# Fused cross-attention and mixture-of-experts kernel: another VectorE order in the attention steps, one undivided row-scatter pair, and batch 15's gate, output and statistics ahead of tile 0

## Chip, cores and metric

One core of one Trainium2 chip runs the kernel. The metric is the device time in microseconds of one execution. All input preparation (transposes, splitting into blocks, constant tables) happens before it.

## What is computed

`x` has 16 batches of 128 tokens with 128 features; a context of the same 16 x 128 tokens has 256 features. Cut to what matters:

```python
x = x + tanh(g_xattn) * xattn(ctx, layernorm(x), mask, mask, W_src, b_src, W_tgt, b_tgt, W_out, b_out)
x = x + tanh(g_ffn) * ffn(layernorm(x), w1, w2, w3, new_w1, new_w2, new_w3, gate, gate_bias)
# xattn: 8 heads of 16, keys and values from ctx, queries from x, masked softmax,
#        then W_out on [layernorm(x), attention result]
# ffn:   scores = sigmoid(x @ gate.T + bias) over 9 experts, the top 2, weights divided by their sum;
#        out = sum over experts of weight * ((silu(x @ w1.T) * (x @ w3.T)) @ w2.T), hidden size 352
```

## The kernel before

The kernel writes every engine's instruction list out by hand and joins the engines with semaphores. It has three stages.

**Projections** (to about 38 us) are not touched.

**Attention steps.** `turns(step)` runs steps k = 0 to 16 on PE, ACT, DVE and POOL; each engine has its own `step(k, r, i)` with r = k mod 4. Step k works on batch k's scores, on batch k-1's probabilities, on batch k-2's output and on batch k-3's normalised rows, so one step carries a quarter of the chain of four batches. On PE (L1189) the order within a step is: score products of batch k (L1178, then the mask bias L1185), `turn_out(k-2)` (L1258), the eight probability transposes of batch k-1 (L1216), `turn_rows(k)` (L1269 and L1275), the products with the values (L1228), and `gate_and_out(k)` (L1283 and L1285). On ACT: two copies of the transposed probabilities, the copy of the turned rows (L448), four exponentials (L405), the copy of the value products (L427), four exponentials.

DVE's step (L877) is, in order: the first row maxima (L829), `unturn` (a reciprocal L835 and a product L839), `norm2` of batch k-3 (L848), the second maxima, then the routing work of the step if there is some, then `second` of batch k-2 (L869, L871, L875: add the output product to x, and the statistics of the layer norm). `norm2(b)` waits for `rs2` of batch b, which POOL makes (L567, L569) from the statistics of `second(b)`.

The **routing** of a group of four batches is spread over steps by `routed(k, r, at)`, which gives group g when k = at + 4g. DVE's parts: `logits_of` and `clamp` at k = 6, 10, 14; `make_keys` and `choose` (`find_top`, `mark_top`: which two experts) at k = 7, 11, 15; `weigh`, `keep_ranks`, `place_rows` and `label_rows` (which row of which expert each token goes to) at k = 8, 12, 16. PE's `rank(g)` (L1234) counts the tokens by expert, inside `turn_rows` at k = 8, 12, 16, behind five or eight filler products (`keep_busy`, L1248). Every small DVE operation of the routing is followed at once by a wait for itself (`route_link`).

POOL's step (L540) is: scale the values of batch k (L545), `rstd2_of(k-3)`, the first copy of a scatter of 128 rows to `x_rows` (L597, for group g and place p at k = 9 + 4g + p), `keep(k-3)` (a copy of the normalised rows, which waits for `norm2`), and the scatter's second copy. `scatter` waits for `label_set` of its group.

**Tables.** `table_counts` and `table_rows` (L923, L948) turn the counts into the row and the expert of each of 40 tiles. `table_rows(0)` for the first 8 tiles runs at k = 14, its `table_counts(0)` at k = 13. After the last step DVE does `unturn(15)`, `norm2(14)`, `table_used(0)` and `table_counts(1)`.

**Tiles.** 40 tiles of 128 rows, each of one expert, run through a pipeline over k: SyncE loads the tile (L299 to L312 for the first eight), PE transposes it (L1334), ACT and DVE split it into two parts, PE multiplies with w1 and w3 (L1323 to L1325), ACT and DVE make the hidden rows, PE transposes and multiplies with w2 (L1374, L1365), ACT scales the result (L477) and POOL scatters it to `y_rows` (L620). The routing of the last group of batches is mixed into tiles 0 to 9 (`within`, `between`). SyncE's list ahead of tile 0 is: wait for `rows_known`, four loads of row numbers into registers (L304), wait for the scatters of the groups before, then the tile loads.

```python
                rows = [sp.value_load(row_of[0:1, n * TR + r:n * TR + r + 1], min_val=0, max_val=NE * CAP) for r in range(AHEAD)]
                for p in range(UN):
                    sp.wait_ge(st_rows[p], (NG - len(EARLY) + n) * 32)
```

Of the kernel before, what the change touches and what calls it, by code (L numbers as in the profile page):

```python
# [18 lines left out]
ALU = mybir.AluOpType  # L19
# [7 lines left out]
P = 128  # L27
NB = 16
# [32 lines left out]
LOWS = {1: (0, 1, 2), 2: (3,), 3: (4,), 4: (5,), 5: (6,), 6: (7,), 9: (8,)}  # L61
# [7 lines left out]
def build(nc, x, ctxT, mask, first, consts, row_consts, w_srcT, w_tgtT, w_outT, w13T, w2T, gateT, x_rows, y_rows, out):  # L69
    with ExitStack() as ctx:  # L70
# [171 lines left out]
        def in_switch(k):  # L242

            return k == SWITCH

# [254 lines left out]
        def _(pool):  # L500
# [39 lines left out]
            def step(k, r, i):  # L540
# [102 lines left out]
        def _(dve):  # L643
# [84 lines left out]
            route_links = {}  # L728
            LINKS = {"clamp": 1, "keys": 4, "choose": 3, "weigh": 4, "place": 2}

            def route_link(g, stage_name, ins):

                route_links[stage_name] = route_links.get(stage_name, 0) + 1
                before = sum(n for name, n in LINKS.items() if list(LINKS).index(name) < list(LINKS).index(stage_name))
                ins.then_inc(route_chain, 1)
                dve.wait_ge(route_chain, g * sum(LINKS.values()) + before + route_links[stage_name])

            def clamp(g):

                route_links.clear()  # L740
                dve.wait_ge(lg_kept, g + 1)
                nc.vector.tensor_scalar(logits[:, 0:GZ], z[:], FLOOR, None, ALU.max).then_inc(lg_ready, 1)
                route_link(g, "clamp", nc.vector.tensor_scalar(key[:].rearrange("p b e -> p (b e)"), z[:], FLOOR, KNEE, ALU.max, ALU.min))
                assert route_links["clamp"] == LINKS["clamp"]

            def add_one(g):

                route_links.clear()
                dve.wait_ge(sig_exp, g + 1)
                route_link(g, "keys", nc.vector.tensor_scalar(sigs[:], sigs[:], 1.0, None, ALU.add))  # L750
                route_link(g, "keys", nc.vector.reciprocal(sigs[:], sigs[:]))

            def above_knee(g):

                knee = sigs[:, GZ:GZ + 1]
                route_link(g, "keys", nc.vector.tensor_scalar(over[:], sigs[:, 0:GZ], knee, knee, ALU.max, ALU.subtract))
                flat_key = key[:].rearrange("p b e -> p (b e)")
                route_link(g, "keys", nc.vector.scalar_tensor_tensor(flat_key, over[:], STRETCH, flat_key, ALU.mult, ALU.add))
                assert route_links["keys"] == LINKS["keys"]

            def make_keys(g):

                add_one(g)
                above_knee(g)

            def find_top(g):

                route_links.clear()
                for b in range(UN):
                    last = nc.vector.max(top[:, b, :], key[:, b, :])  # L770
                route_link(g, "choose", last)
                for b in range(UN):
                    last = nc.vector.max_index(top_at[:, b, :], top[:, b, :], key[:, b, :])
                route_link(g, "choose", last)

            def mark_top(g):

                last = nc.vector.tensor_tensor(choices[:], part["experts"].unsqueeze(1).unsqueeze(1).to_broadcast([P, 2, UN, NE]),
                                               top_at[:, :, 0:2].rearrange("p b c -> p c b").unsqueeze(3).to_broadcast([P, 2, UN, NE]), ALU.is_equal)
                route_link(g, "choose", last)  # L780
                assert route_links["choose"] == LINKS["choose"]
# [3 lines left out]

            def choose(g):

                find_top(g)
                mark_top(g)
# [6 lines left out]
            def weigh(g):  # L796

                route_links.clear()
                dve.wait_ge(chosen, g + 1)
                route_link(g, "weigh", nc.vector.tensor_tensor(flat_of, flat_choices, of_choices(sigs[:, 0:GZ]), ALU.mult))  # L800
                route_link(g, "weigh", nc.vector.tensor_reduce(sel_sig[:], chosen_of[:], AX.X, ALU.add))
# [679 lines left out]
```

## Time and profile before

| What | us |
|---|---|
| median of 3 runs (lowest, highest) | 215.69 (215.64, 215.78) |
| the profiled execution | 215.48 |
| its span, first to last instruction | 213.7 |
| PE, DVE, ACT, POOL busy | 201.5, 147.7, 142.3, 128.4 |
| mean granted TensorE clock | 0.994 of full speed |

The profiled execution lies 0.2 us below the median. Its own time is 1.8 us more than its span. PE's busy time counts matmuls whose ends are modelled, so it also covers short waits.

### The profile page before, as it was taken

Reading aid. Unit: us, or ns where it says so; the run is one execution under the profiler, and the core shown is the slowest. Engines: PE = TensorE matmul, PEld = TensorE weight load, DVE = VectorE, ACT = ScalarE, POOL = GpSimd, SP = SyncE. Lnnn points to the kernel's source line nnn. Section 1 sums busy time; section 2 is a strip of 40 time slices with the busy share of each in tenths; the row PEclk is TensorE's granted clock in tenths of the full one; section 3 lists DMA queues with packets and bytes.
Section 4 is the critical chain, followed back from the end, with each engine's and each line's share of the span. In section 5 each row is a group of like instructions: output and inputs, shape, how many; then the busy total and the mean of one; then the engine's idle time right before and its main releaser. Section 6 shows DMA issues by size and latency. Waiting matters only on the chain.

```text
span 213.7 us, 5788 instructions
## 1 busy us (share of the span) xinstructions
PE 201.5 (94%) x1606; PEld 162.8 (76%) x1606; DVE 147.7 (69%) x523; ACT 142.3 (67%) x399; POOL 128.4 (60%) x230
## 2 busy tenths in 40 slices
PE   8999998999999999999979899999999999999972
PEld 2676575576766676676648789999999999998971
DVE  0269979877889969899977997534444344467583
ACT  2355896999886888678746757576666767666110
POOL 5226657023342588677767867888888887567120
PEclk9999999999999999999999999999999999999997
DMA  5997999999993001000024823232222222261394
GB/s 151 380 391 208 366 408 406 404 398 344 312 349 92 14 28 37 25 28 26 28 70 122 234 64 96 69 87 76 66 77 72 60 64 62 66 225 33 87 354 155
DMA packets 23601, 34.91 MB, mean 163 GB/s; under 512 B 2561, under 2 KB 15878, under 8 KB 23442
## 3 DMA queue, kind: packets, MB, share of 16 engines
q1 hardware_dynamic: 20610, 29.27, 40.9%
q0 software_dynamic: 2240, 4.23, 6.3%
q10 hardware_dynamic: 720, 1.02, 1.6%
q8 instruction: 15, 0.25, 0.5%
q14 instruction: 16, 0.13, 0.2%
HBM read 15.85 MB, written 19.06 MB: 163 GB/s over the span
## 4 chain that ended last, share of the span: by engine, by line
PE 61%; DVE 18%; POOL 6%; issue 5%; ACT 5%; DMA 3%; POOLq 0%; SPq 0%; DVEq 0%; ACTq 0%
PE pt_ps L1365 10%; PE score_ps L1323 5%; PE pt_ps L1374 5%; PE score_ps L1325 5%; PE score_ps L1324 5%; PE score_ps L1178 4%; PE pt_ps L1118 4%; PE ps_a L1228 3%; PE pt_ps L1216 3%; PE score_ps L1128 3%; DVE less L829 2%; DMA kheads<-y_rows 2%; ACT probs L405 2%; PE ps_a L1334 2%; POOL y_rows L620 2%
## 5 line engine op out<-in xcount | busy, mean ns | idle before, releaser
L620 POOL DMA_INDIRECT y_rows<-vals,ids x38 | 37.7, 993 | 11.2 <-ACT vals L477 4.4
L405 ACT ACTIVATE probs<-score_ps,less 128x128 f32<-128x128 f32 x128 | 37.4, 405 | 1.7 <-DVE less L829 1.7
L597 POOL DMA_INDIRECT x_rows<-stage,slot x32 | 32.6, 1020 | 9.2 <-issue 7.7
L1365 PE MATMUL pt_ps<-w,probsT 128*128 x234 | 32.6, 275 | 0.9 <-DVE probsT L1018 0.6
L1365 PEld LDWEIGHTS pt_ps<-w,probsT 128*128 128x128 f32 x234 | 30.8, 190 | 1.6 <-issue 1.4
L477 ACT ACTIVATE vals<-pt_ps,xg 128x128 f32<-128x128 f32 x38 | 13.9, 367 | 26.6 <-PE pt_ps L1365 26.6
L1045 DVE TENSOR_TENSOR xg_low<-ps_a,xg_high 128x128 fp32r<-128x128 f32 x40 | 11.6, 290 | 28.8 <-ACT xg_high L459 28.4
L1323 PE MATMUL score_ps<-w_high,xg_low 128*128 x80 | 29.2, 365 | 0.0
L1325 PE MATMUL score_ps<-w_high,xg_high 128*128 x80 | 25.9, 323 | 0.0
L1324 PE MATMUL score_ps<-w_low,xg_high 128*128 x80 | 25.6, 320 | 0.0
L1053 DVE TENSOR_TENSOR probs<-probs,score_ps 128x352 f32<-128x352 f32 x40 | 20.8, 520 | 6.4 <-ACT probs L466 3.6
L829 DVE TENSOR_REDUCE less<-score_ps 128x4 f32<-128x512 f32 x32 | 21.7, 684 | 3.0 <-PE score_ps L1185 2.9
L466 ACT ACTIVATE probs<-score_ps 128x352 f32<-128x352 f32 x40 | 18.6, 464 | 1.3 <-PE score_ps L1325 1.2
L1374 PE MATMUL pt_ps<-fst,probs 128*128 128x128 f32 x117 | 19.2, 273 | 0.1
L484 ACT COPY probsT<-pt_ps 128x384 f32<-128x384 f32 x38 | 18.2, 478 | 0.3 <-PE pt_ps L1374 0.2
L1178 PE MATMUL score_ps<-kheads,qT 64*128 64x256 f32 x128 | 18.2, 402 | 0.2
L1216 PE MATMUL pt_ps<-fst,probs 128*128 128x128 f32 x128 | 17.1, 274 | 1.0 <-ACT probs L405 1.0
L567 POOL TENSOR_SCALAR ve<-mv 128x1 f32<-128x1 f32 x16 | 3.7, 231 | 22.8 <-DVE mv L875 22.8
L1216 PEld LDWEIGHTS pt_ps<-fst,probs 128*128 128x128 f32 x128 | 14.4, 141 | 2.0 <-ACT probs L405 1.9
L1323 PEld LDWEIGHTS score_ps<-w_high,xg_low 128*128 128x128 f32 x80 | 15.1, 189 | 0.5 <-issue 0.2
L1324 PEld LDWEIGHTS score_ps<-w_low,xg_high 128*128 128x128 f32 x80 | 15.2, 190 | 0.0
L1325 PEld LDWEIGHTS score_ps<-w_high,xg_high 128*128 128x128 f32 x80 | 15.0, 187 | 0.0
(179 smaller groups left out, 442.8 us busy)
## 6 DMA issues: line engine op xcount, KB each, us to landing
x_rows<-pads SPq DMA_DIRECT2D x1, 9945.0 KB, 37.2
w_low<-in_w13T SPq DMA_DIRECT2D x3, 1056.0 KB, 10.5
xg<-x_rows SPq DMA_DIRECT2D x40, 65.0 KB, 1.8
ctx_r<-in_ctxT SPq DMA_DIRECT2D x4, 512.0 KB, 7.1
y_rows<-pads SPq DMA_DIRECT2D x1, 2048.0 KB, 18.1
w<-in_w2T SPq DMA_DIRECT2D x1, 1728.0 KB, 12.6
kheads<-y_rows SPq DMA_DIRECT2D x3, 512.0 KB, 5.2
mask_b<-in_mask SPq DMA_DIRECT2D x4, 256.0 KB, 7.5
```

The costliest lines, as they stand in the source:

```text
L405: last = nc.scalar.activation(probs[:, r % 2, h, :], score_ps[:, r % 2, h, :], ACT.Exp, bias=less[:, r % 2, h:h + 1])
L597: pool.indirect_dma_start(x_rows[:, :], bass.IndirectOffsetOnAxis(ap=slot[:, par, c, p:p + 1], axis=0), stage[:, par, c, p, :], None, boun ...
L620: pool.indirect_dma_start(y_rows[:, :], bass.IndirectOffsetOnAxis(ap=ids[:, s:s + 1], axis=0), yt[:, s, :], None, bounds_check=last_row, o ...
L829: nc.vector.tensor_reduce(less[:, r % 2, here], score_ps[:, r % 2, here, :], AX.X, ALU.max, negate=True).then_inc(lessened, 1)
L1053: nc.vector.tensor_tensor(hid[:, q, :], gated[:, q, :], bank[2 + q][:, 0:HID], ALU.mult).then_inc(hid_done, 1)
L1178: nc.tensor.matmul(score_ps[:, r % 2, half * HH + 2 * pair:half * HH + 2 * pair + 2, :], qT[rows, k * P:(k + 1) * P], kheads[rows, heads, ...
L1216: last = nc.tensor.transpose(pt_ps[:, half, h, :], probs[:, q, half * UN + h, :], ident)
L1323: nc.tensor.matmul(dst[:, 0:HID], xg_low[:, q, :], of(w13_high), start=True, stop=False)
L1324: nc.tensor.matmul(dst[:, 0:HID], xg_high[:, q, :], of(w13_low), start=False, stop=False)
L1325: return nc.tensor.matmul(dst[:, 0:HID], xg_high[:, q, :], of(w13_high), start=False, stop=True)
L1365: last = nc.tensor.matmul(into[:, 0:D], hidT[:, q3, c, :], w2[:, bass.ds(e3, 1), c, :].rearrange("p o d -> p (o d)"), start=(c == 0), stop ...
L1374: last = nc.tensor.transpose(bank[4][:, c * P:(c + 1) * P], hid[:, q2, c0:c0 + P], ident)
```

## The change

The new lists of DVE's step and what follows it; helper functions were split so that each operation waits only for what it reads (`known(name)`), not for the operation just issued:

```diff
             def step(k, r, i):
+                keyed, marked, labelled = routed(k, r, UN + 3), routed(k, r, 2 * UN), routed(k, r, 2 * UN + 1)
+                if labelled is not None:
+                    keep_ranks(labelled)
+                if on(k, 2):
+                    inverse(k - 2, r % 2)
+                    divide(k - 2, r % 2)
+                if keyed is not None:
+                    add_one(keyed)
+                if on(k, 3):
+                    norm2(k - 3)
+                if keyed is not None:
+                    invert(keyed)
                 if on(k, 0):
                     maxima(k, r, 0)
-                if on(k, 2):
-                    unturn(k - 2, r % 2)
-                if on(k, 3):
-                    norm2(k - 3)
+                if keyed is not None:
+                    over_knee(keyed)
+                if labelled is not None:
+                    weigh_and_label(labelled)
                 if on(k, 0):
                     maxima(k, r, 1)
+                if keyed is not None:
+                    stretch(keyed)
+                if marked is not None:
+                    find_top(marked)
+                    find_places(marked)
+                    mark_top(marked)
+                    mark_both(marked)
                 for expert in LOWS.get(k, ()):
                     low(expert)
-                if routed(k, r, UN + 3) is not None:
-                    make_keys(routed(k, r, UN + 3))
-                if routed(k, r, 2 * UN) is not None:
-                    weigh(routed(k, r, 2 * UN))
-                if k == 3 * UN + 1:
+                if k == 3 * UN + 2:
                     table_counts(0)
-                if k == 3 * UN + 2:
-                    table_rows(0)
                 if on(k, 2):
                     dve.wait_ge(o_mm, k - 1)
                     if routed(k, r, UN + 2) is not None:
                         logits_of(routed(k, r, UN + 2))
-                    if routed(k, r, 2 * UN) is not None:
-                        keep_ranks(routed(k, r, 2 * UN))
                     second(k - 2)
-                if routed(k, r, UN + 3) is not None:
-                    choose(routed(k, r, UN + 3))
-                if routed(k, r, 2 * UN) is not None:
-                    place_rows(routed(k, r, 2 * UN))
-                    label_rows(routed(k, r, 2 * UN))
+                if k == NB:
+                    table_rows(0)
...
-            unturn(NB - 1, 1)
+            keep_ranks(NG - 2)
+            inverse(NB - 1, 1)
+            divide(NB - 1, 1)
             norm2(NB - 2)
-            table_used(0)
-            table_counts(1)
+            weigh_and_label(NG - 2)
+            second(NB - 1)
```

`weigh_and_label` issues `pick_slots`, `pick`, `sum_slots`, `sum_picked`, `add_both`, `invert_total`, `store_weights` and `label_rows`. `table_used(0)`, `count_tiles(1)` and `pass_tiles(1)` move into tiles 0, 1 and 2; `second(15)` no longer stands between tiles 0 and 1. Expert 8's `low` moves from step 9 to step 10. On PE:

```diff
+            return (ps_b, 3 * P + GZ) if g == NG - 1 else (ps_a, 2 * P)
...
+            return (b + 1) // UN - 2 if b % UN == UN - 1 and b >= 2 * UN - 1 else None
...
             def turn_out(b):
                 if b == NB - 2:
                     keep_busy(2 * (b % 2), 3)
                 pe.wait_ge(o_copied, b + 1)
+                if ranked_ahead_of(b) is not None:
+                    rank(ranked_ahead_of(b))
...
             def turn_rows(k):
                 if on(k, 2):
-                    if k >= 2 * UN and k % UN == 0:
-                        keep_busy(2 * ((k - 1) % 2), 8 if k == 3 * UN else 5)
                     pe.wait_ge(normed, k - 1)
-                    if routed(k, k % UN, 2 * UN) is not None:
-                        rank(routed(k, k % UN, 2 * UN))
...
             turn_rows(NB + 1)
+            gate_and_out(NB + 1)
...
                     pe.wait_ge(ld_tile[r], i * 16 + 16)
+                    if k == 0:
+                        pe.wait_ge(ranks_kept, NG - 1)
...
             def between(k):
-                if k == 0:
-                    gate_and_out(NB + 1)
```

PE's value products also wait for `ranks_kept` in the step of a rank. On POOL, the last step (k = 16) issues both copies of its scatter before `keep`:

```diff
-                        scatter(routed(k, r, 2 * UN + 1 + p), p, (0,))
+                        scatter(routed(k, r, 2 * UN + 1 + p), p, (0,) if k < NB else (0, 1))
...
-                    if routed(k, r, 2 * UN + 1 + p) is not None:
+                    if routed(k, r, 2 * UN + 1 + p) is not None and k < NB:
                         scatter(routed(k, r, 2 * UN + 1 + p), p, (1,))
```

## Rows read from the trace of the kernel before

**Rows 1.** The page's chain that ended last, shares by engine.
```profile
PE 61%; DVE 18%; POOL 6%; issue 5%; ACT 5%; DMA 3%; POOLq 0%; SPq 0%; DVEq 0%; ACTq 0%
```

**Rows 2.** Timeline: start, length, engine, line; PE's score products of steps 7, 8, 9, 11, 12, 13, 15.
```profile
60.43 1.14 PE L1178 MATMUL score_ps<-kheads,qT 64*128 64x256 f32 x8
...
64.80 1.13 PE L1178 MATMUL score_ps<-kheads,qT 64*128 64x256 f32 x8
...
70.26 1.13 PE L1178 MATMUL score_ps<-kheads,qT 64*128 64x256 f32 x8
...
79.25 1.13 PE L1178 MATMUL score_ps<-kheads,qT 64*128 64x256 f32 x8
...
83.75 1.13 PE L1178 MATMUL score_ps<-kheads,qT 64*128 64x256 f32 x8
...
89.67 1.14 PE L1178 MATMUL score_ps<-kheads,qT 64*128 64x256 f32 x8
...
98.53 1.14 PE L1178 MATMUL score_ps<-kheads,qT 64*128 64x256 f32 x8
```

**Rows 3.** Timeline, steps 11 and 12: the expert choice, the next maxima, PE's filler products.
```profile
84.94 0.35 DVE L770 MAX8 top<-key 128x8 f32<-128x9 f32 x4
...
86.18 1.89 PE L1248 MATMUL score_ps<-ones 128*128 128x512 bf16 x8
...
86.39 0.68 DVE L829 TENSOR_REDUCE less<-score_ps 128x4 f32<-128x512 f32 x1
```

**Rows 4.** Timeline, step 13: the turn-out, then DVE from the reciprocal by norm2 to the second maxima.
```profile
90.95 0.44 PE L1258 MATMUL ps_b<-fst,oT 128*128 128x128 f32 x2
...
91.85 0.19 DVE L835 RECIPROCAL rden<-ps_b 128x8 f32<-128x8 f32 x1
...
92.28 0.34 DVE L848 SCALAR_TENSOR_TENSOR stage<-xs,mv,rs 128x128 f32<-128x128 f32 x1
...
92.54 0.68 DVE L829 TENSOR_REDUCE less<-score_ps 128x4 f32<-128x512 f32 x1
```

**Rows 5.** Timeline, step 12: the first and the last of DVE's six weighing operations.
```profile
88.29 0.22 DVE L800 TENSOR_TENSOR chosen_of<-choices,sigs 128x72 f32<-128x72 f32 x1
...
89.36 0.18 DVE L809 TENSOR_SCALAR stage<-cst 128x8 f32<-128x8 f32 x1
```

**Rows 6.** Timeline, steps 8 to 10: the label, POOL's first scatter, and what stands behind it.
```profile
71.81 0.19 DVE L823 CAST slot<-slot_f 128x8 int32<-128x8 f32 x1
...
72.69 1.22 POOL L597 DMA_INDIRECT x_rows<-stage,slot  x1 [0.34 <-issue]
...
76.43 0.24 POOL L567 TENSOR_SCALAR ve<-mv 128x1 f32<-128x1 f32 x1
...
77.36 0.35 DVE L848 SCALAR_TENSOR_TENSOR stage<-xs,mv,rs 128x128 f32<-128x128 f32 x1
...
77.77 0.14 PEld L1275 LDWEIGHTS ps_b<-fst,stage 128*128 128x128 f32 x1 [0.24 <-DVE stage L848]
```

**Rows 7.** Timeline, step 14: the sixth operation of table_rows(0), which gives the row numbers.
```profile
98.40 0.16 DVE L958 TENSOR_SCALAR row_of<-row_f 1x8 int32<-1x8 f32 x1
```

**Rows 8.** SyncE's line 304 near 101.0: the check behind the fourth register load.
```profile
L304 SPq SEQ_ASSERT  x1: 18/18/18, 101.0 to 101.0; - x1
```

**Rows 9.** Timeline around tile 0, and PE's transpose of tile 8.
```profile
107.05 0.98 POOL L597 DMA_INDIRECT x_rows<-stage,slot  x1 [0.37 <-issue]
...
108.31 0.28 DVE L869 TENSOR_TENSOR xs<-ps_b,xs 128x128 f32<-128x128 f32 x1
...
109.60 6.27 SPq L312 DMA_DIRECT2D xg<-x_rows  x8
...
111.49 0.33 PE L1334 MATMUL ps_a<-fst,xg 128*128 128x128 f32 x1 [0.62 <-DMA xg<-x_rows]
...
128.46 0.27 PE L1334 MATMUL ps_a<-fst,xg 128*128 128x128 f32 x1
```

**Rows 10.** A stretch of 2 us: busy time of PE, PEld, DVE, ACT, POOL, then TensorE's clock.
```profile
210.00:212.00 2.00, 0.00 (x0) 0.00 (x0) 0.51 (x2) 0.00 (x0) 0.00 (x0) 0.76 0.61 214
```

More of the change, by code:

```diff
@@ L726, in _, with route_link @@
                     spread(j)
[L728 to L734, printed above, removed]
+            route_links, made = [0], {}
+            def route_link(name, ins):
+                route_links[0] += 1
@@ L735, in route_link, with known @@
                 ins.then_inc(route_chain, 1)
-                dve.wait_ge(route_chain, g * sum(LINKS.values()) + before + route_links[stage_name])
+                made[name] = route_links[0]
+            def known(name):
+                dve.wait_ge(route_chain, made[name])
+            flat_key = key[:].rearrange("p b e -> p (b e)")
             def clamp(g):
-                route_links.clear()
                 dve.wait_ge(lg_kept, g + 1)
                 nc.vector.tensor_scalar(logits[:, 0:GZ], z[:], FLOOR, None, ALU.max).then_inc(lg_ready, 1)
-                route_link(g, "clamp", nc.vector.tensor_scalar(key[:].rearrange("p b e -> p (b e)"), z[:], FLOOR, KNEE, ALU.max, ALU.min))
@@ L761, in make_keys, with invert, over_knee @@
-            def make_keys(g):
-                add_one(g)
-                above_knee(g)
+                route_link("one_more", nc.vector.tensor_scalar(sigs[:], sigs[:], 1.0, None, ALU.add))
+            def invert(g):
+                known("one_more")
+                route_link("sigs", nc.vector.reciprocal(sigs[:], sigs[:]))
+            def over_knee(g):
+                known("sigs")
+                knee = sigs[:, GZ:GZ + 1]
+                route_link("over", nc.vector.tensor_scalar(over[:], sigs[:, 0:GZ], knee, knee, ALU.max, ALU.subtract))
@@ L766, in find_top, with stretch, find_places @@
+            def stretch(g):
+                known("over")
+                route_link("key", nc.vector.scalar_tensor_tensor(flat_key, over[:], STRETCH, flat_key, ALU.mult, ALU.add))
             def find_top(g):
-                route_links.clear()
+                known("key")
                 for b in range(UN):
                     last = nc.vector.max(top[:, b, :], key[:, b, :])
-                route_link(g, "choose", last)
+                route_link("top", last)
+            def find_places(g):
+                known("top")
@@ L781, in mark_top, with mark_both @@
-                assert route_links["choose"] == LINKS["choose"]
+                route_link("choices", last)
+            def mark_both(g):
+                known("choices")
                 if g >= 1:
@@ L840, in unturn @@
                                         rden[:, q, :].unsqueeze(2).to_broadcast([P, H, HD]), ALU.mult).then_inc(normed, 1)
+            turned = ps_b[:, 0:2 * P].rearrange("p (h c) -> p h c", h=H)
             def norm2(b):
@@ L1020, in within @@
             def within(k):
+                if k == 0:
+                    table_used(0)
+                if k == 1:
+                    count_tiles(1)
+                if k == 2:
+                    pass_tiles(1)
                 if k == SWITCH:
@@ L1026, in within @@
                     add_one(NG - 1)
+                    invert(NG - 1)
                 if k == 4:
-                    above_knee(NG - 1)
+                    over_knee(NG - 1)
+                    stretch(NG - 1)
                 if k == 5:
                     mark_top(NG - 1)
+                    mark_both(NG - 1)
                 if k == 6:
                     keep_ranks(NG - 1)
-                    place_rows(NG - 1)
+                    pick_slots(NG - 1)
+                    sum_slots(NG - 1)
                     label_rows(NG - 1)
@@ L1068, in between @@
             def between(k):
-                if k == 0:
-                    second(NB - 1)
                 if k == 1:
@@ L1331, in tile @@
                     pe.wait_ge(ld_tile[r], i * 16 + 16)
+                    if k == 0:
+                        pe.wait_ge(ranks_kept, NG - 1)
                     if k >= 1:
```

101 lines of the change are left out of this document (60 added, 41 removed).

## The prediction

> **What bounds the kernel now.** I read the chain that ended last first, for the engine that sets the pace, then the timeline of the attention steps, because the change lies there, and last the queues of POOL and SyncE, because the change moves what they wait for. PE carries 61% of the chain [rows 1]. I call S the start of a step's score products. An undisturbed step takes 64.80 - 60.43 = 4.37 us [rows 2], and PE passes from product to product in it. Steps 7 to 14 take 38.10 us from S to S where eight plain ones would take 34.96. The reader should see where the 3.14 us lie: 1.09 in step 8, 0.25 in steps 9 and 10 together (8.99), 0.13 in step 11, 1.55 in step 12, 0.12 in steps 13 and 14 (8.86). Steps 8 and 12 lose it because the expert choice (84.94 to 86.39, 1.45 us) stands ahead of their first maxima, and PE fills the hole with products that nobody needs, eight in 1.89 us [rows 3]. In the tile stage PE sets the pace again: from tile 0 to tile 8 it takes 16.97 us [rows 9], and after that nothing but PE's work spaces the tiles, so a shift at tile 8 stays to the end.
>
> **Steps 8, 12, 7 and 11: the gain.** The filler products go, and the choice moves behind the second maxima of its step. There it must be ready for the rank in the next step's turn-out. The maxima end near S + 3.8, the choice 1.45 later at S + 5.2; PE comes to the rank after the next scores at S + 4.37 + 1.28 = 5.65 (90.95 - 89.67 = 1.28 [rows 2, 4]). It is in time, so both steps fall to 4.37, and step 11 with them: 1.09 + 1.55 + 0.13 = -2.77 us. What is late next is `second` of the choosing step. It waits behind the choice and ends its three operations (0.28 for the first [rows 9], 0.8 as an estimate for all) at S + 6.0. From the statistics POOL's two operations and the start of norm2 take 77.36 - 76.43 = 0.93 [rows 6], so norm2 of the labelled step starts at S + 7.0 or 2.6 to 2.7 into that step.
>
> **Steps 9 and 10, 13 and 14: the loss.** The label of a group moves from the end of step 8 to the middle of step 9 (13 for the next group), while POOL's first scatter of the group stays at step 9 and waits for it. Counted from S of step 9: the turn-out ends at 1.28 + 0.2 for the rank + 0.44 = 1.92 [rows 4]; from the reciprocal by norm2 to the next maxima it is 92.54 - 91.85 = 0.69 [rows 4], which with the late norm2 puts the first maxima at 2.9. They hold VectorE 0.6. Then come nine small operations: the six of weighing took 89.54 - 88.29 = 1.25 [rows 5], three more at the same 0.21 make 1.9 one after another. In the new order neighbours don't need each other; norm2 gives way to the next operation after 0.26 although it lasts 0.34 [rows 4], so I take 0.3 off: 1.6 us, and the label is there at 5.1. The Trainium skill, page "VectorE: DVE Perf Modes", section "The DRAIN you can't avoid", says the opposite of chained operations: leaving the semaphores out saves nothing. By it the term would be 1.9, which makes 0.3 more in each of two places.
>
> Now the queue behind the waiting scatter. In the kernel before the label ended at 72.00 and the scatter began at 72.69, S + 2.43 [rows 2, 6]; it now begins near 5.3. Behind it on POOL stand `keep`, the second copy and the values of the next batch; only then come `ve` and `rs` of the batch before. This stretch took 76.43 - 72.69 = 3.74 [rows 6]. Its parts alone (two scatters of 0.98 to 1.22 [rows 6, 9], two short operations) make an estimated 2.9; I take 3.0, near the sum of the parts, since nothing else has to stand there, and keep 3.74 for the range. So `ve` starts at 8.3, though its statistics are ready at 6.5. norm2 starts 0.93 later at 9.2, PE's turned rows 0.41 after that (77.77 - 77.36), and the next score products but one 79.25 - 77.77 = 1.48 after those [rows 2, 6]: S + 11.1 for two steps. The rows show that this path is live: in step 10 PE's weight load already waits 0.24 for norm2's output [rows 6]. Cost: 11.1 - 8.99 = +2.1 and 11.1 - 8.86 = +2.2 us. The bounds of each are +1.7 (2.9 on POOL, label at 4.9) and +2.8 (3.74). The first maxima now stand behind norm2, but ScalarE's exponentials wait for PE's turned rows anyway, which norm2 holds just as long: no price, unless something else comes between. Expert 8's `low` in step 10 and `table_counts(0)` in step 14 lie beside this wait, with VectorE idle; if POOL were on time they would delay `second` by some 0.4 and 0.9. At step 15 the kernel is at -2.77 + 2.1 + 2.2 = **+1.5 us**.
>
> **From step 15 to tile 0.** Before, this took 111.49 - 98.53 = 12.96 [rows 2, 9]. The sum x + output of batch 14 began at S + 9.78 (108.31). Five fillers go (0.236 each [rows 3], -1.2), and `add_one` and `invert` now stand ahead of step 15's first maxima, and so of the exponentials and all behind them (+0.6): S + 9.2. Then `second` ends (0.8) and `table_rows(0)` follows, which was in step 14 before, where it was covered by PE's products. Its first six operations, at 0.16 to 0.21 each with their waits, are an estimated 1.1, so the row numbers are known at S + 11.1. SyncE's four register loads wait for them: before they ran from 98.56 to 101.0, 2.46 us [rows 7, 8], while SyncE had nothing else to wait for until 109.60 [rows 9]. Now they are bare. With 0.2 to the issue, tile 0's load goes out at S + 13.8 and lands 111.49 - 109.60 = 1.89 later [rows 9]: 15.7 against 12.96, **+2.7 us**. The bounds are +1.9 (VectorE reaches the table 0.8 earlier) and +3.5. The unbroken scatter pair brings its second copy forward by some 0.6; in the kernel before that copy set the loads (107.05 to 109.60, 2.55 us [rows 9]), but now its data lands before S + 11, nearly 3 us ahead of the register loads. I cost it at 0; with the table in time it would be worth 0.6.
>
> **Tiles 0 to 8.** Batch 15's gate, output and `second` leave the ramp (about 0.6 on PE, 0.8 on VectorE); `table_used`, counts and passes of the second table, eleven operations, come between tiles 0 and 2, where VectorE mostly waits for ScalarE. I take -0.5 of the 16.97 us, bounds -1.0 and +0.5. Group 2's label is also later by about the whole shift, so its eight scatters and tile 8's load move with it.
>
> **Sum.** 1.5 + 2.7 - 0.5 = +3.7 us on the profiled execution's 215.48: 219.2. The median of the runs lies 0.2 higher, so I expect **219.4 us**.
>
> **The rivals.** (a) POOL absorbs the late label: if `ve` of steps 10 and 14 starts by the time its statistics are ready (S + 6.5, so the scatter by S + 3.5), the gain of 2.77 stands: -2.77 + 2.7 - 0.5 = -0.6, 215.1 us, **faster**. Against it: the label's own path of 5.1 is longer than 3.5 by any reading of the rows. 7%. (b) The late loads are partly paid back in the ramp, where 16.97 us for eight tiles held slack for work that VectorE now has done: -2.0 in place of -0.5 gives +2.2, 217.9. 12%. (c) Group 2's scatters land later than the shift and tile 8 waits for its load, 1.0 to 2.0 on top: 220.9. 8%. (d) The clock. TensorE was granted 0.76 of its full rate in the stretch in which PE had no product at all [rows 10], which means that it fell there from 2.4 to 1.2 GHz. The change takes the fillers away and leaves holes of nearly 2 us in steps 10 and 14 and ahead of tile 0. If the rate falls there, two tiles (2.1 us each) at half rate cost another 4.2: 223.6. For it speaks that the fillers stood at such holes; against it that the holes are short and the span's mean is 0.994. The Trainium skill, page "TensorE: Matmul & The Clock Gate", section "What's actually happening", has activity release the throttle and idleness bring it back, which is this rival. 7%. (e) Gain and loss meet, or the order is no order in effect: 215.7. 3%.
>
> **How the numbers follow.** My forecast has 63%. The range takes in (b), (c) and the bounds of the two POOL terms and the table term, 217.3 to 221.3; (a), (d), (e) are left out. A difference of 0.2% is about what a measurement of this kernel can tell from no change. Slower by more than that: forecast, (b), (c), (d), 90%; within 3%; faster 7%.
>
> **What the changed profile should show.** Steps 8 and 12 near 4.4 us and steps 9 + 10, 13 + 14 near 11; POOL idle for the label before the first scatter of a group, `ve` following v_cur without a wait; VectorE's norm2 released by POOL and PE's turned rows by VectorE; SyncE's register loads directly ahead of the first tile load, and PE released by that load at tile 0, near 115.7. I am wrong if steps 9 + 10 stay below 9.5, or if the first tile load goes out before the register loads have been on the path.

## The result and the profile after

| | Kernel before | Changed kernel |
|---|---|---|
| median (lowest, highest), 4 runs each on one chip | 215.66 us (215.52, 215.78) | 223.75 us (223.38, 224.20) |
| the profiled execution, its span | 215.48, 213.7 | 223.83, 222.0 |
| mean granted TensorE clock | 0.994 | 0.956 |

The ratio is 1.0395, 95% interval 1.0364 to 1.0426: the change costs 8.1 us. The forecast was 219.4 with a range up to 221.3, so its direction was right and its size was not. In the experiments below, medians and ranges hold every execution unless said otherwise, and a ratio leaves out those over 1.5% above the fastest of the same kernel.

The page of the changed kernel: PE's busy time, the granted clock in 40 slices of 5.55 us, the chain that ended last by engine, and the group of the row scatters.

```profile
PE 203.4 (92%) x1588; PEld 165.6 (75%) x1588; DVE 144.3 (65%) x523; ACT 142.2 (64%) x399; POOL 128.4 (58%) x230
...
PEclk9999999999999969995895899999999999999997
...
PE 71%; DVE 10%; ACT 5%; issue 5%; POOL 5%; SPq 1%; DMA 1%; POOLq 0%; ACTq 0%; DVEq 0%
...
L605 POOL DMA_INDIRECT x_rows<-stage,slot x32 | 33.3, 1039 | 17.5 <-DVE slot L854 10.3
```

PE's share of the chain rose from 61% [rows 1] to 71%, although the change takes filler products away, and its busy time from 201.5 to 203.4 us with 18 products fewer. More time for less work points at a slower PE, and the second line says so: a slice of 6, then 5 and 8, then 5 and 8 again stand in the middle of the span. The last line says that POOL sits idle for 10.3 us in all for the labels of four groups, of which 2.68 and 2.65 us lie in steps 9 and 13.

Timeline of the changed kernel, which answers to [rows 2]: the score products of steps 8, 9, 11, 12, 13 and 15.

```profile
63.93 1.14 PE L1259 MATMUL score_ps<-kheads,qT 64*128 64x256 f32 x8
...
68.30 1.14 PE L1259 MATMUL score_ps<-kheads,qT 64*128 64x256 f32 x8
...
79.60 2.08 PE L1259 MATMUL score_ps<-kheads,qT 64*128 64x256 f32 x8
...
85.55 1.14 PE L1259 MATMUL score_ps<-kheads,qT 64*128 64x256 f32 x8
...
89.92 1.14 PE L1259 MATMUL score_ps<-kheads,qT 64*128 64x256 f32 x8
...
101.91 2.08 PE L1259 MATMUL score_ps<-kheads,qT 64*128 64x256 f32 x8
```

Steps 8 and 12 take 4.37 us, as forecast. Steps 11 and 15, each the one behind a long wait, open with the same eight products in 2.08 us where the others need 1.14. Busy time and clock by stretch show the same (columns: PE, PEld, DVE, ACT, POOL busy, granted clock, DMA share, GB/s):

```profile
75.00:80.00 5.00, 2.76 (x30) 1.97 (x30) 2.53 (x5) 2.77 (x9) 4.34 (x8) 0.95 0.13 42
80.00:83.00 3.00, 3.00 (x15) 1.90 (x14) 1.25 (x9) 1.33 (x6) 2.70 (x5) 0.51 0.08 24
83.00:86.00 3.00, 2.86 (x33) 2.08 (x33) 2.70 (x9) 2.57 (x9) 2.31 (x4) 1.00 0.09 29
...
100.00:107.00 7.00, 7.00 (x42) 5.06 (x36) 4.85 (x23) 3.73 (x13) 4.62 (x9) 0.51 0.09 30
107.00:115.00 8.00, 7.08 (x71) 4.13 (x70) 5.98 (x37) 6.07 (x16) 4.80 (x8) 1.00 0.09 28
...
117.00:124.00 7.00, 4.20 (x14) 3.84 (x15) 3.20 (x15) 1.54 (x5) 5.69 (x8) 0.51 0.46 104
```

There are three spells (stretches at the lower clock, 1.2 instead of 2.4 GHz), of about 3.4, 6.8 and 6.8 us. The first two begin 1.4 and 0.4 us behind the end of a wait of PE of over 2 us (the first near 79.5, the second near 100), the third within PE's wait for tile 0's rows. PE is 100% busy in the first two: a reader who looks only at busy time would call these stretches perfect.

The waits themselves, in step 10 (this answers to [rows 6]): label, first scatter, `ve`, norm2, PE's turned rows; the last line is PE's turned rows in step 14.

```profile
73.16 0.17 DVE L854 CAST slot<-slot_f 128x8 int32<-128x8 f32 x1
...
73.64 1.23 POOL L605 DMA_INDIRECT x_rows<-stage,slot  x1 [2.68 <-DVE slot L854]
...
76.78 0.24 POOL L575 TENSOR_SCALAR ve<-mv 128x1 f32<-128x1 f32 x1
...
77.72 0.35 DVE L894 SCALAR_TENSOR_TENSOR stage<-xs,mv,rs 128x128 f32<-128x128 f32 x1 [2.47 <-POOL rs L577]
...
78.12 0.33 PE L1356 MATMUL ps_b<-fst,stage 128*128 128x128 f32 x1 [2.21 <-DVE stage L894]
...
99.60 0.33 PE L1356 MATMUL ps_b<-fst,stage 128*128 128x128 f32 x1 [2.03 <-DVE stage L894]
```

Counted from S of step 9 (68.30) the scatter starts at 5.34, `ve` at 8.48, norm2 at 9.42 and step 11 at 11.30; the forecast had 5.3, 8.3, 9.2 and 11.1. And the tail, which answers to [rows 7, 9]: the row numbers, the first tile loads, tile 0 and tile 8.

```profile
114.22 0.16 DVE L1024 TENSOR_SCALAR row_of<-row_f 1x8 int32<-1x8 f32 x1
...
117.18 3.01 SPq L320 DMA_DIRECT2D xg<-x_rows  x5
...
119.03 0.48 PE L1418 MATMUL ps_a<-fst,xg 128*128 128x128 f32 x1 [2.04 <-DMA xg<-x_rows]
...
136.91 0.27 PE L1418 MATMUL ps_a<-fst,xg 128*128 128x128 f32 x1
```

From the row numbers to the load 117.18 - 114.38 = 2.80 us pass with nothing else on the path: the four register loads, bare. The last scatter of group 1 had ended at 113.02, so it did not hold the load.

### The profile page after: what moved, and what is told of

Its sections match the earlier page's. It is cut to its first block, busy times and chain, and to the rows that moved or that the text cites. A ratio compares the mean times of both kernels' runs of the same rounds, so it can differ in the third digit from the quotient of the medians.

```text
span 222.0 us, 5746 instructions
## 1 busy us (share of the span) xinstructions
PE 203.4 (92%) x1588; PEld 165.6 (75%) x1588; DVE 144.3 (65%) x523; ACT 142.2 (64%) x399; POOL 128.4 (58%) x230
## 4 chain that ended last, share of the span: by engine, by line
PE 71%; DVE 10%; ACT 5%; issue 5%; POOL 5%; SPq 1%; DMA 1%; POOLq 0%; ACTq 0%; DVEq 0%
PE pt_ps L1449 12%; PE score_ps L1405 6%; PE score_ps L1407 6%; PE score_ps L1406 6%; PE pt_ps L1458 6%; PE score_ps L1259 6%; PE pt_ps L1297 4%; PE ps_a L1311 4%; PE pt_ps L1199 3%; PE score_ps L1209 2%; PE ps_a L1418 2%; ACT probs L413 2%; POOL x_rows L605 2%; PE ps_b L1343 2%; PE ps_b L1366 2%
## 5 line engine op out<-in xcount | busy, mean ns | idle before, releaser
L605 POOL DMA_INDIRECT x_rows<-stage,slot x32 | 33.3, 1039 | 17.5 <-DVE slot L854 10.3
L1405 PE MATMUL score_ps<-w_high,xg_low 128*128 x80 | 30.0, 375 | 0.0
L1407 PE MATMUL score_ps<-w_high,xg_high 128*128 x80 | 26.4, 330 | 0.0
L1406 PE MATMUL score_ps<-w_low,xg_high 128*128 x80 | 26.3, 328 | 0.0
L871 DVE TENSOR_REDUCE less<-score_ps 128x4 f32<-128x512 f32 x32 | 20.7, 676 | 0.2 <-PE score_ps L1266 0.2
L1259 PE MATMUL score_ps<-kheads,qT 64*128 64x256 f32 x128 | 20.0, 436 | 0.2
L1297 PE MATMUL pt_ps<-fst,probs 128*128 128x128 f32 x128 | 18.7, 287 | 1.0 <-ACT probs L413 1.0
L1458 PE MATMUL pt_ps<-fst,probs 128*128 128x128 f32 x117 | 19.2, 273 | 0.0
L1297 PEld LDWEIGHTS pt_ps<-fst,probs 128*128 128x128 f32 x128 | 15.5, 149 | 2.5 <-ACT probs L413 2.5
L1405 PEld LDWEIGHTS score_ps<-w_high,xg_low 128*128 128x128 f32 x80 | 15.6, 195 | 0.5 <-issue 0.2
L1406 PEld LDWEIGHTS score_ps<-w_low,xg_high 128*128 128x128 f32 x80 | 15.8, 197 | 0.1
```

Source lines behind the costliest of these rows:

```text
L605: pool.indirect_dma_start(x_rows[:, :], bass.IndirectOffsetOnAxis(ap=slot[:, par, c, p:p + 1], axis=0), stage[:, par, c, p, :], None, boun ...
L871: nc.vector.tensor_reduce(less[:, r % 2, here], score_ps[:, r % 2, here, :], AX.X, ALU.max, negate=True).then_inc(lessened, 1)
L1259: nc.tensor.matmul(score_ps[:, r % 2, half * HH + 2 * pair:half * HH + 2 * pair + 2, :], qT[rows, k * P:(k + 1) * P], kheads[rows, heads, ...
L1297: last = nc.tensor.transpose(pt_ps[:, half, h, :], probs[:, q, half * UN + h, :], ident)
L1405: nc.tensor.matmul(dst[:, 0:HID], xg_low[:, q, :], of(w13_high), start=True, stop=False)
L1406: nc.tensor.matmul(dst[:, 0:HID], xg_high[:, q, :], of(w13_low), start=False, stop=False)
```

## The experiments

**Theory A**: the waits are those of the forecast (POOL behind the label, the late table), some 3.7 us, and the rest is the clock that falls in the holes they leave. **Theory B**: the waits alone are the loss, twice as large as forecast, and the low clock only accompanies them. Eleven kernels were run, in four sets; each set had the kernel before on its own chip (215.05, 215.19, 215.18 and 215.08 us). "Fillers" below are the kernel's own products that compute nothing (`keep_busy`), so they change no output.

**1. Fillers in the holes.** In the changed kernel:

```diff
                     last = nc.tensor.transpose(ps_b[:, 0:P], upd[:, k % 2, :], ident)
+                    if k in (2 * UN + 2, 3 * UN + 2):
+                        keep_busy(2 * ((k - 1) % 2), 8)
...
             gate_and_out(NB + 1)
+            keep_busy(0, 8)
```

> The changed kernel with filler products put into its three holes: eight in steps 10 and 14 behind the turned output rows, where PE waits for norm2, and eight ahead of tile 0. They compute nothing that is used. Theory A (the waits for the label and for the row numbers cost about 3.7 us, as forecast, and the rest of the 8.1 us is TensorE's lower clock that follows the holes): the granted clock stays at its full level through steps 9 to 15 and the first tiles, and the time falls to 219.3, within 0.6. Theory B (the waits themselves were priced too low, and the spells at the lower clock lie where PE has time to spare): the clock may rise, but the time stays above 222.5.

Measured: 220.15 us (219.89 to 220.54), ratio 1.0231 (1.0174 to 1.0289), clock 0.989 to 0.992. Extra work on the busiest engine took 3.0 us off the loss: the kernel is 5.1 us behind the kernel before on its own chip, where the change without fillers is 8.1 behind. (The medians, 220.15 and 223.75, come from two chips.) Theory B needed more than 222.5; theory A's 219.3, within 0.6, was missed by 0.25. Steps 9 and 10 take 11.30 as without fillers, so the wait is untouched, but step 11 falls from 5.95 to 4.62. One spell is left, ahead of tile 0 (same columns):

```profile
110.00:114.00 4.00, 2.68 (x14) 1.51 (x15) 3.64 (x23) 1.04 (x2) 1.03 (x3) 1.00 0.05 17
114.00:117.00 3.00, 3.00 (x11) 1.10 (x8) 0.77 (x3) 0.00 (x0) 2.45 (x4) 0.58 0.38 85
```

Before the clock falls PE was busy for 2.68 of 4 us, and its longest wait there was 0.83; the eight fillers stand behind that and run at the lower clock themselves.

**2. Fillers in every hole.** As 1, but 9 products for 5 behind the last turn-out, 3 behind batch 15's turned rows and 12 ahead of tile 0:

```diff
             turn_out(NB - 1)
-            keep_busy(0, 5)
+            keep_busy(0, 9)
             turn_rows(NB + 1)
+            keep_busy(0, 3)
             gate_and_out(NB + 1)
+            keep_busy(0, 12)
```

> The changed kernel with products that compute nothing in every hole of the attention tail: 8 in steps 10 and 14, 9 in place of 5 behind the last turn-out, 3 behind the turned rows of batch 15, 12 ahead of tile 0. Theory A (the changed kernel's loss is the waits of the forecast plus spells at the lower clock): no half-rate stretch at all, granted clock 0.99 or more, steps as in the run with fewer such products (9 and 10 about 11.3, 13 and 14 about 11.4), S15 to tile 0 about 16, tiles 0 to 8 about 16.3, time 219.0 to 219.8, which is what was forecast for the change without the clock. Rival (the clock falls for a reason that products do not touch, or the products themselves delay PE's work): clock below 0.985 or time above 220.2.

Measured: 220.06 us (219.86 to 220.36), ratio 1.0236 (1.0206 to 1.0266), clock 0.988 to 0.997. The page's clock row has no spell left, and the starts of steps 13 and 15 and of tiles 0 and 8 are:

```profile
PEclk9999999999999999999999999999999999999998
...
89.12 1.13 PE L1259 MATMUL score_ps<-kheads,qT 64*128 64x256 f32 x8
...
100.53 1.14 PE L1259 MATMUL score_ps<-kheads,qT 64*128 64x256 f32 x8
...
116.65 0.27 PE L1422 MATMUL ps_a<-fst,xg 128*128 128x128 f32 x1
...
132.95 0.27 PE L1422 MATMUL ps_a<-fst,xg 128*128 128x128 f32 x1
```

This is the change at full clock: +4.9 us on the kernel before, against +8.1 with the clock left to itself. Theory B is out. The time stays within 0.3 us of run 1, though one more spell is gone (my bound of 219.8 was missed by 0.3): the spell of run 1 lay on fillers, where PE had only tile 0's rows to wait for. A spell costs little where PE does not set the pace.

**3. Each scatter one step later** in the changed kernel, so that POOL does not meet the label's wait; group 1's last pair goes behind the steps:

```diff
-                    if routed(k, r, 2 * UN + 1 + p) is not None:
-                        scatter(routed(k, r, 2 * UN + 1 + p), p, (0,) if k < NB else (0, 1))
+                    if routed(k, r, 2 * UN + 2 + p) is not None:
+                        scatter(routed(k, r, 2 * UN + 2 + p), p, (0,) if k < NB else (0, 1))
...
             rstd2_of(NB - 2)
+            scatter(NG - 3, UN - 1)
```

(the second copies likewise).

> The changed kernel with each of POOL's row scatters issued one step later (k = 10 + 4g + p), so that the first one finds its label already there. Theory A: steps 9 + 10 and 13 + 14 fall from 11.3 and 12.0 us to about 9.0 each, no hole is left there, the clock stays full up to step 16, and the time is 216.5 to 217.5, since the row numbers still come late. Theory B: the steps fall as much, but nothing else comes with them: 219 or more. A third reading (POOL was not what held norm2): the steps stay near 11 and the time at 223.

Measured: 220.82 us (220.31 to 221.13), ratio 1.025 (1.0191 to 1.0308): above theory A's 217.5 and on theory B's side of 219, but the trace says why. Steps 9 and 10 fall from 11.30 to 9.36, 13 and 14 from 11.99 to 9.86, and no spell follows either: POOL's wait was the hole. A part of it moves to step 11, which takes 5.19 us with a wait of 1.01 for norm2. The tail gives the rest back (S15 to tile 0 17.33, tiles 0 to 8 18.21): group 1's last pair, now behind the steps, ends at S15 + 13.67 and the first load goes out 1.65 us later, so PE waits 3.59 us for tile 0's rows, and a spell of 6.8 us begins within that wait.

**4. The late table alone, in the kernel before:**

```diff
-                if k == 3 * UN + 2:
-                    table_rows(0)
...
                     second(k - 2)
+                if k == NB:
+                    table_rows(0)
```

> The kernel before with table_rows(0) moved from step 14 to step 16 behind second(14), as in the change, and nothing else. If SyncE's four register loads behind it are then on the path, the first tile load goes out near 113.0 in place of 109.6 and tile 0 starts 3.4 us later: 218 to 219.5 with the clock full, 1 to 2 more if the hole ahead of tile 0 brings it down. If the ramp of the tiles had room for it, 216.5 or less.

Measured: 219.11 us (218.62 to 219.39), ratio 1.0182 (1.0126 to 1.0238), clock 0.979 to 0.984. Eight small operations moved two steps cost 4.1 us. Row numbers, first load, tile 0:

```profile
109.08 0.16 DVE L958 TENSOR_SCALAR row_of<-row_f 1x8 int32<-1x8 f32 x1
...
112.03 3.01 SPq L312 DMA_DIRECT2D xg<-x_rows  x5
...
114.05 0.42 PE L1334 MATMUL ps_a<-fst,xg 128*128 128x128 f32 x1 [2.89 <-DMA xg<-x_rows]
```

Again 112.03 - 109.24 = 2.79 us of register loads; S15 to tile 0 is 16.25 against 12.96, and tiles 0 to 8 are 0.7 longer, because the clock falls around the 2.89 us of waiting (0.77 from 112 to 116).

**5. Only the fillers gone, in the kernel before:**

```diff
-                    if k >= 2 * UN and k % UN == 0:
-                        keep_busy(2 * ((k - 1) % 2), 8 if k == 3 * UN else 5)
```

> The kernel before without the five, eight and five filler products of steps 8, 12 and 16, and nothing else changed. PE then waits 1.1 to 1.4 us for the output rows in each of these steps. Theory A says that the clock is what the fillers buy: if holes of this length bring it down, the time rises by 1 to 4 us to 217 to 220; if they are too short for it, the fillers themselves cost 0.3 us in steps 12 and 16 each and the time falls to 215.0. Theory B: no change of the clock matters, 215.0.

Measured: median 216.13 us, ratio 1.0039 (1.0006 to 1.0073). Here the holes are shorter; in step 12 PE waits 1.32 us for `upd`:

```profile
87.42 0.19 PE L1238 MATMUL ps_b<-both,rows_below 128*128 128x36 bf16 x1 [1.32 <-DVE upd L839]
```

In the profiled execution no spell follows, and step 12 is even 0.23 shorter than with fillers (5.69 against 5.92). But the ten executions differ: five took 215.1 to 215.6 us at a mean clock of 0.985 to 0.999, three 216.7 to 217.0 at 0.984 to 0.986, two 218.5 and 218.6 at 0.970 and 0.977. Thirteen of the kernel before on the same chip took 214.5 to 216.6 at 0.986 to 0.999. The slower ones have the lower clock, but none of them was profiled: that their clock fell behind these holes is likely and not shown. In the trace the fillers of the kernel before cost 0.2 to 0.3 us; they look like an insurance against executions up to 3.5 us longer.

**6. table_rows(0) one step earlier, in the changed kernel** (`if k == NB` becomes `if k == NB - 1`):

> The changed kernel with one edit: table_rows(0) stands one step earlier, in step 15 behind `second`, so that the eight row numbers are known about 4 us sooner. Theory A (waits and clock, the late table being the largest wait ahead of tile 0): S15 to tile 0 falls from 17.12 us to 13.5 to 14.5, then set by the last row scatter; the half-rate spell of step 14 stays, the one at the tail goes or shortens; time 219.0 to 220.5. Rival theory (POOL's late scatters of group 1 hold tile 0 anyway, as every one of them was pushed back by the late label): the first tile load moves by less than 1 us, 222.8 or more. If table_rows(0) itself in step 15 delays `second` of the next steps, S15 to tile 0 falls but the time by under 2 us.

Measured: 220.11 us (219.06 to 223.23), ratio 1.0191 (1.0162 to 1.0221): again a time that goes with the clock, 219.1 to 219.2 at 0.986, 221.0 and 221.3 at 0.970 and 0.963, 223.2 at 0.955. The time lies in the band of theory A, but the profiled execution was the slowest, with S15 to tile 0 at 15.05, above the 13.5 to 14.5 expected, so this run could not say what held the tile at full clock. Run 7 does.

**7. The same at full clock** (run 2 with the table in step 15 and without the 12 fillers ahead of tile 0):

> The run with the clock held by products that compute nothing, with one more edit: table_rows(0) in step 15 (and the 12 products ahead of tile 0 left out, whose hole it closes). Theory A (of the 3.2 us that S15 to tile 0 is longer than before at full clock, the late table is all, since the last scatter of group 1 ends 9.5 us behind S15 in both): S15 to tile 0 falls from 16.12 to 13.0 to 13.8, time 217.0 to 217.8 (220.06 without the edit). Rival (the scatters or batch 15's gate and output hold tile 0 as well): S15 to tile 0 stays above 14.8, time above 218.7.

Measured: 218.02 us (217.78 to 218.31), ratio 1.0126 (1.01 to 1.0152), so 2.0 us under run 2 and 0.2 above the expected band. Row numbers, group 1's last scatter, first load, tile 0:

```profile
107.25 0.16 DVE L1024 TENSOR_SCALAR row_of<-row_f 1x8 int32<-1x8 f32 x1
...
108.95 0.97 POOL L605 DMA_INDIRECT x_rows<-stage,slot  x1 [0.30 <-issue]
...
111.49 3.01 SPq L320 DMA_DIRECT2D xg<-x_rows  x5
...
114.24 0.30 PE L1421 MATMUL ps_a<-fst,xg 128*128 128x128 f32 x1
```

The load goes out at S15 + 10.99; in the kernel before it was 109.60 - 98.53 = 11.07. So the table was all that made it late; the last scatter sets it again, 1.57 us behind its end in both (111.49 - 109.92, 109.60 - 108.03). Tile 0 itself stands at S15 + 13.74, 0.8 later than before, since PE first does batch 15's gate and output and some fillers.

**8. The unbroken pair alone, in the kernel before:**

```diff
-                        scatter(routed(k, r, 2 * UN + 1 + p), p, (0,))
+                        scatter(routed(k, r, 2 * UN + 1 + p), p, (0,) if k < NB else (0, 1))
```

(and `and k < NB` at the second copy).

> The kernel before with one part of the change alone: in step 16 both copies' scatters go out ahead of `keep`. In the kernel before the second scatter of that pair (107.05) set the first tile load (109.60). Theory A (it does): the load goes out 0.5 to 0.6 us earlier, tile 0 starts 0.5 earlier, time 0.2 to 0.3% below the kernel before beside it (214.4 to 214.6 where that gives 215.05). Rival (the load is set by something else, or the tiles behind wait for the weights or rows of others): no difference within 0.1%.

Measured: 215.27 us over 12 runs, ratio 1.0005 (0.9987 to 1.0023). A miss for theory A's line: the second scatter does start earlier (S15 + 8.15 against 8.52), the load by 0.22 and tile 0 with them (12.67 against 12.96), but tiles 0 to 8 take 17.24 instead of 16.97, and S15 to tile 8 is 29.91 against 29.93. A tile 0 that comes 0.3 us early is worth nothing.

**9. Both waits repaired**: run 3's later scatters, but group 1's last pair in step 16; the table in step 15; 4 fillers in steps 10 and 14 and ahead of tile 0.

> The changed kernel with both of its late waits repaired: each row scatter one step later so that POOL never waits for the label (the last two pairs of group 1 both in step 16), table_rows(0) in step 15, and 4 products that compute nothing in steps 10 and 14 and ahead of tile 0 for the clock. Theory A (the new VectorE order is worth its 2.8 us once POOL is not blocked): steps 8 to 14 take 33.2 us or less as in the run with later scatters (33.73 in the kernel before), S15 to tile 0 13.0 to 14.0, tiles 0 to 8 16.3 to 17, time 214.3 to 216.0, so near the kernel before. Rival (later scatters hold the first tile load: four in step 16 take 4.3 us from the values of step 16 on): S15 to tile 0 above 15, time 217 or more. Rival with the clock: a half-rate spell stays in step 14 or at the tail, 217 to 219.

Measured: 216.4 and 216.5 us at clock 0.995 and 0.994, 220.05 and 220.06 at 0.974 and 0.973; theory A's 214.3 to 216.0 was not reached. S15 to tile 0 is 15.29 (13.0 to 14.0 expected), above the 15 that the rival named, and the load goes out 1.70 us behind the last of the four scatters in step 16. PE waits for norm2's rows behind these scatters too (the row, then two stretches in the columns above):

```profile
110.41 0.33 PE L1360 MATMUL ps_b<-fst,stage 128*128 128x128 f32 x1 [2.04 <-DVE stage L896]
...
108.00:110.40 2.40, 0.37 (x3) 0.02 (x1) 0.40 (x2) 0.00 (x0) 1.89 (x4) 1.00 0.17 56
110.40:114.00 3.60, 2.35 (x12) 1.42 (x13) 2.58 (x15) 0.64 (x3) 1.67 (x2) 1.00 0.37 93
```

In this execution, one of the two short ones, a wait as long as those of the changed kernel was followed by no spell at all. Steps 8 to 14 took 97.32 - 63.90 = 33.42 us, just above my 33.2: the four fillers in steps 10 and 14 now stood in the way of these steps, which took 5.28 and 5.46 us against 4.78 and 4.97 in run 3.

**10. POOL's order repaired by halves.** In the label steps POOL does everything else first and waits for the label with one scatter behind it; the table is in step 15:

```diff
+            HALVES = {10: (0, 1, 3), 11: (0, 3, 5), 12: (0, 5, 7), 13: (0, 7, 8), 14: (1, 1, 3), 15: (1, 3, 5), 16: (1, 5, 8)}
...
+                if k < NB and k not in (10, 14):
+                    values(k)
                 if on(k, 3):
                     rstd2_of(k - 3)
+                if k in HALVES:
+                    halves(*HALVES[k])
                 if on(k, 3):
                     keep(k - 3)
+                if k in (9, 13):
+                    values(k + 1)
+                    halves(k // 4 - 2, 0, 1)
```

> The changed kernel with POOL's order repaired by halves and table_rows(0) in step 15. In the two label steps POOL first does everything else (`keep`, the values of the next step) and then waits for the label with a single scatter behind it; the second copy goes into the next step behind ve and rs, and so on; three scatters in step 16. No products are added. Theory A (the wait for the label costs only through what is queued behind it on POOL): steps 9 and 10, 13 and 14 fall to 9.0 to 9.6 us, there is no hole in steps 10 and 14 and so no half-rate spell there; S8 to S15 about 32.5 (33.73 in the kernel before); S15 to tile 0 13.5 to 14.2 (one more scatter in step 16 than before); tiles 0 to 8 16.3 to 17; time 214.3 to 216.0 with the clock at 0.99. Rival (the late label holds PE by VectorE's own order, not by POOL): steps 9 and 10 above 10.5. Rival of the clock: a spell at the tail as in the run with table_rows(0) early and four scatters in step 16, 217 to 220.

Measured: 217.17 us (216.52 to 218.65; 214.3 to 216.0 expected), ratio 1.0078 (1.005 to 1.0105), clock 0.98 to 0.99. POOL's label step now reads:

```profile
74.98 1.22 POOL L613 DMA_INDIRECT x_rows<-stage,slot  x1 [1.63 <-DVE slot L862]
...
76.24 0.24 POOL L583 TENSOR_SCALAR ve<-mv 128x1 f32<-128x1 f32 x1
...
77.17 0.35 DVE L902 SCALAR_TENSOR_TENSOR stage<-xs,mv,rs 128x128 f32<-128x128 f32 x1 [0.58 <-POOL rs L585]
```

The label is as late as ever, yet from the scatter to `ve` only 1.26 us pass instead of 3.14, norm2's wait falls from 2.47 to 0.58, and steps 9 and 10 take 9.54, 13 and 14 9.67. Step 11 takes 4.79. S8 to S15 is 32.74 against 33.73 in the kernel before. S15 to tile 0 is 15.17 (13.5 to 14.2 expected), with three scatters in step 16, and a spell follows (0.50 from 114 to 118).

**11. The same with fillers at the tail** (8 for 5, then 3, then 4 ahead of tile 0):

> The run with POOL's order repaired by halves and table_rows(0) in step 15, and with products that compute nothing at the tail only (8 in place of 5 behind the last turn-out, 3 behind batch 15's turned rows, 4 ahead of tile 0). Theory A (what that run still loses against its own steps is one half-rate spell between tiles 0 and 8): granted clock 0.99 or more in every run, tiles 0 to 8 fall from 18.56 to 16.3 to 17, S15 to tile 0 stays near 15, time 215.0 to 216.2 with a spread under 0.6 us. So the new VectorE order would be level with the kernel before and not ahead of it, because its 1.0 us of shorter steps is given back by POOL, whose last scatters stand 1.4 us later behind S15. Rival (the spell has another cause than PE's idle time): clock still 0.98, 216.5 to 218.7 from run to run.

Measured: 216.01 us, ratio 1.0024 (1.0002 to 1.0045); every clock at 0.992 or more. Eleven of the twelve executions took 215.00 to 216.71; the twelfth took 659.85 us at a clock of 1.0, and nothing recorded says why. S8 to S15 is 32.77, S15 to tile 0 14.68, tiles 0 to 8 16.52: 63.97 in all, against 63.66 before. The spread of the eleven was 1.7 us, not the 0.6 I expected. So the new VectorE order with both waits and the clock repaired is level with the old one or slightly behind. No version was found that beats the kernel before.

## Why the prediction was wrong

S8 to tile 8, by stretch (us); the third column is the change as it is, the last is run 2, the change at full clock:

| Stretch | Before | Forecast | Measured | At full clock |
|---|---|---|---|---|
| step 8 | 5.46 | -1.09 | -1.09 | -1.09 |
| steps 9, 10 | 8.99 | +2.1 | +2.31 | +2.31 |
| step 11 | 4.50 | -0.13 | +1.45 | +0.11 |
| step 12 | 5.92 | -1.55 | -1.55 | -1.55 |
| steps 13, 14 | 8.86 | +2.2 | +3.13 | +2.55 |
| S15 to tile 0 | 12.96 | +2.7 | +4.16 | +3.16 |
| tiles 0 to 8 | 16.97 | -0.5 | +0.91 | -0.67 |
| sum | 63.66 | +3.7 | +9.32 | +4.82 |

The medians show 8.1 where the sum says 9.3; the changed kernel's profile reached S8 0.87 us earlier (63.93 against 64.80 [rows 2]), ahead of every changed step.

**The failed step is rival (d), the clock**, which the prediction put at 7% and left out of the range, "against it that the holes are short and the span's mean is 0.994". The mean was that of a kernel whose holes were filled; it could not speak for one without fillers, and in run 5, without fillers, five of the ten executions took 1.1 us or more above the other five, at a mean clock of 0.970 to 0.986, though no trace shows where. Leaving the clock out is 4.5 us (9.32 - 4.82) of the 5.6 by which the sum was short; on the medians it is 3.2 (8.1 less 4.9), as the executions also differ in how early they reach S8. The rival named the three holes rightly (2.21, 2.03 and 2.04 us), and its price, +4.2 on two tiles at half rate, was near in size and mostly wrong in place: against full clock, 1.34 of the 4.5 fell on step 11, 0.58 on steps 13 and 14, 1.00 between S15 and tile 0 and 1.58 on the first tiles. That its 223.6 lies so near 223.75 is partly luck: the clock took less than 4.2 on the medians, and the waits more than 3.7. The rule that the prediction cites from the Trainium skill, page "TensorE: Matmul & The Clock Gate", section "What's actually happening", that idleness brings the throttle back, agrees with the trace: 0.51 in three stretches in or behind waits of 2.2, 2.0 and 2.0 us. How long a wait must be is not shown: run 9 has one of 2.04 us with no spell, run 1 a spell behind waits of 0.83 and less.

**Steps 8 and 12** were right to 0.01. **Step 11** was not: the 0.13 did not come; it is 4.61 at full clock where 4.37 was expected; what holds the 0.24 was not tried. **The range** did not quite follow from its own bounds: both POOL terms and the table term at their bounds give 217.7 and 221.5, where it says 217.3 and 221.3, and the lower POOL bound is +1.8 by its parts and not +1.7. Neither end reaches what was measured.

**The label and POOL's queue** were right as a mechanism and in size: label at S + 5.03 (5.1), scatter to `ve` 3.14 (3.0 taken, 3.74 as the bound). Runs 3 and 10 remove that wait in two ways, and 1.6 to 1.9 us of each pair of steps go with it (11.30 to 9.36 and 9.54; 11.41 at full clock to 9.86 and 9.67); step 11 behind them gives back 0.58 and 0.18 (5.19 and 4.79 against 4.61). The term for steps 13 and 14 was 0.35 too small. The nine small operations took 71.86 to 73.33, 1.47 us, near the 1.6 taken from the trace. The Trainium skill's page "VectorE: DVE Perf Modes", section "The DRAIN you can't avoid", has it that chained operations gain nothing from leaving the semaphores out, which would have made 1.9 of the rows; here independent operations were interleaved, and that did save time.

**The table and the register loads** were right: load at S15 + 13.8 forecast, 13.87 in run 2, run 4 shows it alone, and run 7 takes it back. The 0.4 on top at full clock are run 2's own twelve fillers, which end behind the landing (S15 + 15.76, if the load takes the 1.89 us of before). That the pair is worth nothing held too, but my "0.6 with the table in time" fell in run 8.

**The ramp** at full clock is -0.67 (forecast -0.5); **rivals (a), (b), (c) and (e)** did not occur: POOL absorbed nothing, tile 8 never waited for its load.

## What to carry to other kernels

Before a filler product or any other cover is removed, price the clock and not only the hole: a wait of PE that costs 2 us can cost another 1 to 2 us in the stretch behind it, and a mean clock near 1 says nothing of the same kernel with its holes opened. When a producer is made later, look at what is queued behind the first consumer that waits for it on an in-order engine; letting that engine do its other work first and wait last took back 1.8 of the 2.3 us that the late producer cost in its two steps (1.6 with the step behind them). And a small chain that is hidden (eight operations and four register loads) is to be moved only together with what it feeds.

## What was not expected

- The kernel of run 5, with waits of 0.7, 1.1 and 1.3 us where the fillers had stood, took 215.1 us in some executions and 218.6 in another, with a lower mean clock in the longer ones. Such a kernel has no single time, and its profile may show the good case.
- The length of a wait alone did not say whether the clock would fall: 2.04 us in run 9 brought no spell, 0.83 in run 1 did, and the two other executions of run 9 had a mean clock of 0.97.
- The spells of the changed kernel last 3.4, 6.8 and 6.8 us, and most of that lies on the work behind a hole, when PE is busiest; where one falls on fillers ahead of a wait (run 1 against run 2) it costs 0.3 us or less.
- A first tile that starts 0.3 us earlier (run 8) changed nothing eight tiles on.
